# Four buffers instead of two for the routed experts' loads and stores, loads issued six blocks ahead

## The chip, the cores and the metric

The kernel runs on one core of a Trainium2 chip. A core has TensorE (PE: matrix products, into PSUM banks), VectorE (DVE), ScalarE (ACT), GpSimd (POOL) and SyncE (SP), which here only issues DMAs, and 16 DMA engines that serve all queues. Engines run their own instruction lists and wait for each other by semaphores. The metric is the device time of one launch in microseconds. Before the change it is 1456.23 us, the median of 3 runs (1455.55 to 1457.21).

## What is computed

One transformer block on x of shape 32 x 256 x 128 (32 sequences, 8192 tokens), float32. The modulation comes from c. First a gated linear attention with 16 heads adds to x, then a mixture of experts with 8 routed experts (top 2 per token) and one shared expert. Cut to what matters here:

```
h = layernorm(x) * (1 + cb) + sb
shared   = (silu(h @ shared_gate.T) * (h @ shared_up.T)) @ shared_down.T
probs    = sigmoid(h @ router_w.T + routing_bias)
scores, indices = top_k(probs, 2);  scores = scores / sum(scores)
w[t, indices[t]] += scores[t]
g = silu(h @ gate_w[e]);  u = h @ up_w[e]
combined = sum over e of  w[:, e] * ((g * u) @ down_w[e])
x = x + gb * (shared + combined)
```

Hidden size H = 128, expert width I = 256. Only a token's two chosen experts have a weight other than zero, and the kernel computes only those.

## The kernel before, in words

**Attention and routing (to about 1062 us).** The attention runs over 32 sequences. Behind it the routing of a pair of sequences at a time normalises, scores and picks the two experts, and POOL scatters each token's row (128 values of h, the token's slot and a mark) with indirect DMAs into rows_dram, which has a region for every expert. SP waits for all of these scatters before it goes on. `ga_all` holds the attention's output gate for all sequences; POOL's `update_x` is its last reader.

**The block table (1062 to 1076 us).** DVE works out, from how many rows each expert has received, a table of 39 blocks of 512 rows (`BLOCKS` = 2 x 8192 / 512 + 7): for every block the expert and the first row. SP reads it with register loads. Blocks beyond an expert's rows hold padding.

**The routed experts, 39 blocks.** All engines run the same pipeline over the blocks, and each has its own loop, whose body has two blocks (`two_units` on ACT and DVE):

- SP: `load_rows(i)` reads the block's row number and loads 260 KB of rows into `erows`; `load_gate_up(i)` reads the expert and loads gate and up weights (128 KB each) into `ew_in`; `load_down(i)` loads the down weights (128 KB) into `ed_in`. `load_ahead(i)` issues rows i+2, gate and up i+2, down i+1. The row load waits for `s_hx` and `s_yr` of block i (transposed, row numbers read), the gate and up load for `s_ewl` of block i, the down load of i+1 for `s_dn` of block i-1 (its down projection is done). These waits are L323.
- PE: `rows_transposed(i+2)` (four transposes, L1315), `gate_up_block(i+1)` (twelve products of 512 columns, three passes of split float32, L1318 to L1320), `down_block(i)` (L1580).
- ACT: `high_weights` and `high_h` round weights and rows to the high part, `silus` applies silu, `copy_y_out` (L814) copies the down projection's PSUM bank to `y_out`, once the scatter that last used that half has landed.
- DVE: `split_block` computes the low parts and the row numbers (`y_rows`, L1235), `gate_times_up` multiplies (L1228), `y_rows_out` (L1242) converts the row numbers into `y_row`, once the scatter two blocks back has landed.
- POOL: `scatter_y(i)` waits for `s_yo` and `s_id` and issues four indirect DMAs (L635) that write 128 rows each into y_dram.

Every buffer that a load or a store touches has two halves: `erows`, `ew_in`, `ed_in`, `y_out`, `y_known` and `y_row`. They lie in `pairs`, which the attention has left by then. The halves for PSUM banks, for the split parts and for `act` are two as well.

**The shared expert (from about 1370 us).** 16 steps of 512 tokens. SP waits until all scatters to y_dram have landed (L426), then loads the rows of y back, DVE combines them with the shared expert's result, POOL applies the gate and adds to x, SP stores.

The order of the work is written out by hand; there is no planner.

Of the kernel before, what the change touches and what calls it, by code (L numbers as in the profile page):

```python
# [21 lines left out]
BLOCKS = TOP * TOKENS // STEP + E - 1  # L22
# [12 lines left out]
def block_kernel(nc, x, W_q, W_k, W_v, W_gate, b_gate, W_o, shared_gate, shared_up, shared_down,  # L35
# [11 lines left out]
    with ctx:  # L47
# [3 lines left out]
        def sem(name):  # L51
# [31 lines left out]
        gb_all = sb("gb_all", [P, B, D])  # L83
        h_all = sb("h_all", [P, TOKENS])
# [20 lines left out]
        block_rows = sb("block_rows", [P, REGION // STEP])  # L105
# [19 lines left out]
        past_blocks = shared[:, 512:512 + BLOCKS * E].rearrange("p (i e) -> p i e", e=E)  # L125
        filled = shared[:, 1024:1024 + E * (REGION // STEP)].rearrange("p (e m) -> p e m", e=E)
# [38 lines left out]
        y_known = sb("y_known", [P, 2, ST])  # L165
        y_row = sb("y_row", [P, 2, ST], i32)
# [37 lines left out]
        s_ce, s_cs, s_cT_ps, s_cT = sem("c_exp"), sem("c_silu"), sem("cT_psum"), sem("cT_ready")  # L204
        s_mod_ps, s_mod = sem("mod_psum"), sem("mod_ready")
# [5 lines left out]
        s_whi, s_wsplit, s_guhi, s_gusplit = sem("w_high"), sem("w_split"), sem("gu_high"), sem("gu_split")  # L211
# [28 lines left out]
        s_rin, s_win, s_din, s_ysc, s_yin = ([sem(f"{n}_{u}") for u in range(2)] for n in (  # L240
            "rows_in", "weights_in", "down_in", "y_scattered", "y_loaded"))
# [8 lines left out]
        (s_xr, s_fc, s_fz, s_fst, s_fmv, s_fve, s_frs, s_fxn, s_fT, s_fh, s_fw, s_fp, s_fa, s_fq, s_fs, s_fb,  # L250
         s_fcl, s_fv, s_fqs, s_fo, s_fot, s_fy, s_fyg, s_fx) = (sem("seq_" + n) for n in (
            "x_reloaded", "selectors", "zeros", "stats", "moments", "variance_eps", "rstd", "xn", "xT_psum", "h",
# [8 lines left out]
        AGAIN = ROUNDS  # L261

# [4 lines left out]
        def _(sp):  # L267
# [118 lines left out]
            def load_rows(i, u):  # L386
                if not (isinstance(i, int) and i < 2):
                    alone(s_hx, i - 1)
                    alone(s_yr, i - 1)
                row = sp.value_load(block_i[0:1, 0, ds(i, 1)], min_val=0, max_val=ROWS - STEP)  # L390
                sp.dma_start(erows[:, u, :, :], rows_dram[ds(row, STEP), :].rearrange("(p n) c -> p n c", p=P)).then_inc(s_rin[u], 16)

            def load_gate_up(i, u):
                if not (isinstance(i, int) and i < 2):
# [5 lines left out]
            def load_down(i, u):  # L400
                if not (isinstance(i, int) and i < 2):
# [4 lines left out]
            for i in range(2):  # L406
                load_rows(i, i)
                load_gate_up(i, i)
            load_down(0, 0)

            def load_ahead(i, u):
                load_rows(i + 2, u)
                load_gate_up(i + 2, u)
                load_down(i + 1, 1 - u)

            load_ahead(0, 0)
            load_ahead(1, 1)
# [3 lines left out]
            load_ahead(BLOCKS - 3, 0)  # L421
            load_down(BLOCKS - 1, 0)

            sp.wait_ge(s_ysc[0], 64 * (BLOCKS // 2 + 1))
            sp.wait_ge(s_ysc[1], 64 * (BLOCKS // 2))
# [25 lines left out]
        def _(pool):  # L451
# [34 lines left out]
            counted(block_rows[:, :], [[STEP, REGION // STEP]], 0, 0).then_inc(s_const, 1)  # L486
# [117 lines left out]
            with growing(pool):  # L604
# [11 lines left out]
                with pool.Fori(0, B) as b:  # L616
                    alone(s_fmv, b + 1)
                    g.tensor_scalar(veps[:, :], mv[:, :, 1], EPS, None, ALU.add).then_inc(s_fve, 1)
                    alone(s_fve, b + 1)
# [10 lines left out]
            def scatter_y(v, u):  # L630

                alone(s_yo, v + 1)
                alone(s_id, v + 1)
                for n in range(ST):
# [4 lines left out]
            with pool.Fori(0, BLOCKS // 2) as k:  # L639
                scatter_y(k * 2, 0)  # L640
                scatter_y(k * 2 + 1, 1)
            scatter_y(BLOCKS - 1, 0)
# [17 lines left out]
        def _(sc):  # L660
            a = nc.scalar
            sc.wait_ge(s_c, 16)
            a.activation(c_e, c_in, ACT.Exp, scale=-1.0).then_inc(s_ce, 1)
# [50 lines left out]
            for k, m in enumerate(W_ORDER):  # L714
# [5 lines left out]
                if k == 2:  # L720
                    sc.wait_ge(s_mod, 1)
                    h_attention(0, 1)
# [66 lines left out]
            def high_weights(v, u, k):  # L789
                if not (isinstance(k, int) and k == 0):  # L790
                    sc.wait_ge(s_u, v * 2 - 2)
                sc.wait_ge(s_win[u], k * 32 + 32)
                a.activation(ew_hi[:, u, :, :].rearrange("p m n -> p (m n)"), ew_in[:, u, :], ACT.Copy).then_inc(s_ewh, 1)

            def high_h(v, u, k):
                sc.wait_ge(s_hx, v + 1)
                if not (isinstance(k, int) and k == 0):
                    sc.wait_ge(s_u, v * 2 - 2)
                a.activation(eh_hi[:, u, :], HX[u][:, :], ACT.Copy).then_inc(s_ehh, 1)
# [5 lines left out]
            def silus(v):  # L805
                for i in range(IT):
                    sc.wait_ge(s_g, v * 2 + i + 1)
                    a.activation(silu[:, i, :], GU[i][0][:, :], ACT.Silu).then_inc(s_silu, 1)

            def copy_y_out(v, u, k):  # L810
                sc.wait_ge(s_dn, v + 1)
                if not (isinstance(k, int) and k == 0):
                    sc.wait_ge(s_ysc[u], k * 64)
                a.activation(y_out[:, u, :, :], DN[u][:, :].rearrange("p (n d) -> p n d", n=ST), ACT.Copy).then_inc(s_yo, 1)  # L814

            high_weights(0, 0, 0)
            high_h(0, 0, 0)
            high_weights(1, 1, 0)
            high_h(1, 1, 0)
            silus(0)  # L820

            def two_units(k):
                high_weights(k * 2 + 2, 0, k + 1)
                high_h(k * 2 + 2, 0, k + 1)
                silus(k * 2 + 1)
                copy_y_out(k * 2, 0, k)
                high_weights(k * 2 + 3, 1, k + 1)
                high_h(k * 2 + 3, 1, k + 1)
                silus(k * 2 + 2)
                copy_y_out(k * 2 + 1, 1, k)  # L830

            two_units(0)
            with sc.Fori(1, BLOCKS // 2 - 1) as k:
                two_units(k)
            high_weights(BLOCKS - 1, 0, BLOCKS // 2)
            high_h(BLOCKS - 1, 0, BLOCKS // 2)
# [819 lines left out]
```

## Time and profile before

| | |
|---|---|
| median of 3 runs | 1456.23 us (1455.55 to 1457.21) |
| profiled execution, its own time | 1459.87 us |
| its span | 1458.10 us |
| granted TensorE clock, mean | 0.957 |
| busy: PE, PEld, DVE, ACT, POOL | 89%, 74%, 75%, 56%, 64% |

The profile is one execution. Its page cuts the span into 40 slices of 36.5 us and gives the busy tenths of each engine:

```profile
PE   6999999999999999999999999999138767787796
DVE  8888889898898988989898998987133433433387
ACT  5666666666666666666666676665023333333342
POOL 3444776867677686776867677676725555555555
PEclk9999999999999999999999999999559988989898
```

A digit of 9 is 90% busy or more. Slices 1 to 28 are attention and routing, slice 29 and part of 30 the block table and the first loads, slices 31 to 37 the routed experts, the last ones the shared expert. PEclk is the clock that TensorE was granted, in tenths of full speed. SPq is SP's own queue of instructions: in the chain of waits a line SPq is time that SP spent in that instruction, "issue" time for which the profile shows no one waited for, "remote" or "another core or an unknown queue" a release whose origin the profile doesn't name. A window's row has start:end, its length, busy us (and number) of PE, PEld, DVE, ACT and POOL, the mean granted clock, the share of the DMA engines, and GB/s.

### The profile page before, as it was taken

How to read it: one execution, taken by the hardware profiler on the slowest of the kernel's cores; microseconds unless marked ns; L12 is line 12 of the kernel's file. 1: busy time of each engine (PE TensorE's matmuls, PEld its weight loads, DVE VectorE, ACT ScalarE, POOL GpSimd, SP SyncE). 2: the span in 40 equal slices, each digit the busy share in tenths (PEclk: the TensorE clock that was granted, in tenths of full speed). 3: DMA queues.
4: the chain of work that ended last, by engine and by line, in shares of the span. 5: the costliest groups of instructions: out<-in, count | busy, mean ns of one | idle time of the engine just before them, and what ended most of it. 6: DMA issues, size and time to landing. Idle time of an engine off the chain costs nothing.

```text
span 1458.1 us, 38072 instructions
## 1 busy us (share of the span) xinstructions
PE 1298.9 (89%) x10935; PEld 1072.5 (74%) x10935; DVE 1094.8 (75%) x3120; ACT 812.4 (56%) x2061; POOL 927.0 (64%) x1426
## 2 busy tenths in 40 slices
PE   6999999999999999999999999999138767787796
PEld 5888788888888788888878888787027656676686
DVE  8888889898898988989898998987133433433387
ACT  5666666666666666666666676665023333333342
POOL 3444776867677686776867677676725555555555
PEclk9999999999999999999999999999559988989898
DMA  8902020202112020220202112020224434443154
GB/s 240 259 7 81 2 96 0 95 16 78 40 55 95 6 89 20 75 90 5 95 15 80 34 61 95 4 92 23 103 81 125 130 114 125 122 124 117 50 168 144
DMA packets 94721, 118.46 MB, mean 81 GB/s; under 512 B 9668, under 2 KB 60535, under 8 KB 94672
## 3 DMA queue, kind: packets, MB, share of 16 engines
q1 hardware_dynamic: 85584, 100.93, 22.1%
q0 software_dynamic: 9088, 16.94, 3.5%
q8 instruction: 23, 0.38, 0.1%
q14 instruction: 26, 0.21, 0.1%
HBM read 50.13 MB, written 61.08 MB: 76 GB/s over the span
## 4 chain that ended last, share of the span: by engine, by line
PE 50%; DVE 22%; issue 13%; SPq 7%; POOL 2%; DMA 2%; DVEq 1%; ACT 1%; another core or an unknown queue 1%; POOLq 0%; ACTq 0%
PE head_banks L1394 10%; PE bank L1405 8%; PE bank L1415 6%; DVE pairs L1048 5%; PE bank L1318 5%; PE bank L1319 5%; PE bank L1320 5%; DVE pairs L1044 4%; DVE A L1070 3%; DVE pairs L1053 2%; SPq L384 2%; PE bank L1356 2%; PE bank L1357 2%; PE bank L1358 2%; DVE xn L887 1%
## 5 line engine op out<-in xcount | busy, mean ns | idle before, releaser
L635 POOL DMA_INDIRECT y_dram<-pairs,y_row x156 | 155.0, 994 | 147.3 <-issue 124.9
L1318 PE MATMUL bank<-h_hi,big 128*128 128x256 f32 x768 | 237.2, 309 | 3.4 <-DVE h_lo L895 2.8
L1044 DVE TENSOR_TENSOR_SCAN pairs<-pairs 128x128 f32<-128x128 f32 x512 | 232.2, 494 | 4.4 <-issue 1.7
L1394 PE MATMUL head_banks<-pairs 64*128 64x128 f32 x2048 | 225.9, 297 | 5.3 <-DVE A L1070 3.2
L1405 PE MATMUL bank<-A,shared 128*64 128x256 f32 (+1 forms) x2048 | 223.0, 339 | 0.0
L1048 DVE TENSOR_TENSOR_SCAN pairs<-pairs,cap 128x128 f32<-128x128 f32 x512 | 219.8, 469 | 0.0
L1319 PE MATMUL bank<-h_lo,big 128*128 128x256 f32 x768 | 216.8, 282 | 0.0
L1320 PE MATMUL bank<-h_hi,big 128*128 128x256 f32 x768 | 216.4, 282 | 0.0
L463 POOL TENSOR_SCALAR_AFFINE_SELECT A<-A 128x256 f32<-128x256 f32 x256 | 113.7, 444 | 154.5 <-ACT A L744 153.4
L1394 PEld LDWEIGHTS head_banks<-pairs 64*128 64x128 f32 x2048 | 155.6, 186 | 62.6 <-issue 42.5
L1070 DVE COPY_PREDICATED A<-causal,head_banks 128x384 f32<-128x384 int32 x256 | 150.2, 587 | 63.4 <-PE head_banks L1394 62.2
L541 POOL TENSOR_SCALAR pairs<-pairs 128x256 f32<-128x256 f32 x256 | 118.0, 461 | 102.5 <-ACT pairs L674 99.7
L744 ACT ACTIVATE A<-head_banks 128x384 f32<-128x384 f32 x256 | 125.3, 490 | 101.9 <-PE head_banks L1394 101.8
L1415 PE MATMUL bank<-wo,shared 128*128 128x128 f32 x1024 | 182.0, 300 | 0.0
L1405 PEld LDWEIGHTS bank<-A,shared 128*64 128x64 f32 x2048 | 124.2, 136 | 67.9
L534 POOL DMA_INDIRECT rows_dram<-token_rows,dest x128 | 130.5, 1019 | 58.2 <-issue 48.1
L1415 PEld LDWEIGHTS bank<-wo,shared 128*128 128x128 f32 x1024 | 133.4, 190 | 43.7 <-issue 43.7
L1318 PEld LDWEIGHTS bank<-h_hi,big 128*128 128x128 f32 x768 | 146.0, 190 | 4.9 <-DVE h_lo L895 3.2
L1319 PEld LDWEIGHTS bank<-h_lo,big 128*128 128x128 f32 x768 | 145.8, 190 | 0.0
L1320 PEld LDWEIGHTS bank<-h_hi,big 128*128 128x128 f32 x768 | 145.5, 189 | 0.0
L688 ACT ACTIVATE shared<-bank 128x256 f32<-128x256 f32 x256 | 98.4, 384 | 65.4 <-PE bank L1405 61.2
L674 ACT ACTIVATE pairs<-bank,half_bg 128x256 f32<-128x256 f32 x256 | 120.1, 469 | 21.6 <-PE bank L1320 8.5
(193 smaller groups left out, 2816.3 us busy)
## 6 DMA issues: line engine op xcount, KB each, us to landing
rows_dram<-pad_row SPq DMA_DIRECT2D x17, 2080.0 KB, 8.2
pairs<-rows_dram SPq DMA_DIRECT2D x39, 260.0 KB
pairs<-y_dram SPq DMA_DIRECT2D x16, 512.0 KB, 3.8
pairs<-in_L_ffn_gate_w_dram SPq DMA_DIRECT2D x39, 128.0 KB
pairs<-in_L_ffn_up_w_dram SPq DMA_DIRECT2D x39, 128.0 KB
pairs<-in_L_ffn_down_w_dram SPq DMA_DIRECT2D x39, 128.0 KB
token_rows<-new_rows SPq DMA_DIRECT2D x16, 260.0 KB, 2.3
mod_rows<-mod_rows_dram SPq DMA_DIRECT2D x32, 128.0 KB, 3.2
```

The source lines that it names most:

```text
L534: g.indirect_dma_start(rows_dram, bass.IndirectOffsetOnAxis(ap=dest[:, m:m + 1], axis=0), token_rows[:, m % PT, :], None, bounds_check=ROW ...
L635: g.indirect_dma_start(y_dram, bass.IndirectOffsetOnAxis(ap=y_row[:, u, n:n + 1], axis=0), y_out[:, u, n, :], None, bounds_check=TOKENS * ...
L744: a.activation(A[:, p % 2, 1, :, :], S[:, 1, 0:3 * P].rearrange("p (c t) -> p c t", c=3), ACT.Copy).then_inc(s_ax, 1)
L1044: v.tensor_tensor_scan(F[:, par, cols], ga_t[:, par, cols], ga_t[:, par, cols], 1.0, ALU.mult, ALU.min)
L1048: ins = v.tensor_tensor_scan(G[:, par, cols], gi_t[:, par, cols], cap[:, :], 1.0, ALU.mult, ALU.min)
L1070: v.copy_predicated(A[:, p % 2, 0, :, :].rearrange("p c t -> p (c t)"), causal[:, :, :].bitcast(i32).rearrange("p c t -> p (c t)"), S[:, 0 ...
L1318: t.matmul(dst, hi, m_hi, start=True, stop=False)
L1319: t.matmul(dst, hi, m_lo, start=False, stop=False)
L1320: return t.matmul(dst, lo, m_hi, start=False, stop=True)
L1394: last = t.matmul(S[:, h, c * P:(c + 1) * P], keys[rows, :], queries[rows, :], start=True, stop=True)
L1405: last = t.matmul(O[h * DK:(h + 1) * DK, k * P:T], v_sb[:, k, vcols], blocks.rearrange("p c t -> p (c t)"), start=(k == 0), stop=(k == CHU ...
L1415: last = t.matmul(Y[:, k * D:(k + 1) * D], oT[:, p % 2, k * P:(k + 1) * P], wo[:, p, :], start=(p == 0 and k == 0), stop=(p == PAIRS - 1), ...
```

## The change

The block size gets a name of its own, `BLOCK`, and stays at 512. Everything that a block loads or stores has four buffers (`RING` = 4) in place of two: `erows`, `ew_in`, `ed_in`, `y_out`, `y_known`, `y_row`, with four semaphores each for loads and scatters. `erows` and `ed_in` move from `pairs` into `ga_all`. What is split, multiplied or kept in PSUM keeps its two halves (`half` = j % 2). A helper `unit(k, j)` names block k * 4 + j, its ring place, its half and how often the place was used before. The loop bodies of all five engines cover four blocks.

SP's loads for rows, gate and up are issued six blocks ahead of the down projection that the same point of the list waits for, the down weights four; a load waits until block i-4, which used its buffer last, is done with it. The first six blocks' rows, gate and up weights and the first four down weights are issued one after the other. To stay within the number of semaphores, some short chains of steps that had a semaphore for each step share one (the modulation, the split of the shared expert's weights, the moments in the branch for growing states). The core of the diff:

```
+BLOCK = 512
+RING = 4
-        ew_in = pairs[:, 0:1024].rearrange("p (u n) -> p u n", u=2)
-        ed_in = pairs[:, 1024:1536].rearrange("p (u i d) -> p u i d", u=2, i=IT)
-        erows = pairs[:, 1536:2576].rearrange("p (u n c) -> p u n c", u=2, n=ST)
-        y_out = pairs[:, 2576:3600].rearrange("p (u n d) -> p u n d", u=2, n=ST)
+        ew_in = pairs[:, 0:2048].rearrange("p (u n) -> p u n", u=RING)
+        y_out = pairs[:, 2048:2048 + RING * BT * D].rearrange("p (u n d) -> p u n d", u=RING, n=BT)
+        after = ga_all[:, :, :].rearrange("p b d -> p (b d)")
+        erows = after[:, 0:RING * BT * ROW].rearrange("p (u n c) -> p u n c", u=RING, n=BT)
+        ed_in = after[:, 3072:4096].rearrange("p (u i d) -> p u i d", u=RING, i=IT)
...
+        TURNS = (BLOCKS - 3) // RING
+        def unit(k, j):
+            return k * RING + j, j % RING, j % 2, k + j // RING
+        def begun(turn):
+            return not (isinstance(turn, int) and turn == 0)
...
-            def load_rows(i, u):
-                if not (isinstance(i, int) and i < 2):
-                    alone(s_hx, i - 1)
-                    alone(s_yr, i - 1)
+            def load_rows(k, j):
+                i, u, _, turn = unit(k, j)
+                if begun(turn):
+                    alone(s_hx, i - (RING - 1))
+                    alone(s_yr, i - (RING - 1))
...
-                    alone(s_ewl, i - 1)
+                    alone(s_ewl, i - (RING - 1))
...
-                    alone(s_dn, i - 1)
+                    alone(s_dn, i - (RING - 1))
...
-            with sp.Fori(1, BLOCKS // 2 - 1) as k:
-                load_ahead(k * 2, 0)
-                load_ahead(k * 2 + 1, 1)
+            for i in range(RING):
+                load_rows(0, i)
+                load_gate_up(0, i)
+                if i >= 1:
+                    load_down(0, i - 1)
+            load_down(0, RING - 1)
+            for i in (RING, RING + 1):
+                load_rows(0, i)
+                load_gate_up(0, i)
+            with sp.Fori(0, TURNS - 1) as k:
+                for j in range(RING):
+                    load_rows(k, j + RING + 2)
+                    load_gate_up(k, j + RING + 2)
+                    load_down(k, j + RING)
...
-                if not (isinstance(k, int) and k == 0):
-                    alone(s_ysc[u], k * 64)
+                if begun(turn):
+                    alone(s_ysc[u], turn * 16 * BT)
```

The last pair is `y_rows_out` on DVE; `copy_y_out` on ACT changes in the same way. PE's `rows_transposed`, `gate_up_block` and `down_block` keep their order: rows of block v+2, gate and up of v+1, down of v.

## Rows read from the trace of the kernel before

**Rows 1.** Windows: length, busy time by engine (columns told above), PEclk, DMA, GB/s.

```profile
1094.00:1376.00 282.00, 220.52 (x1245) 189.71 (x1244) 108.24 (x226) 105.51 (x194) 155.00 (x156) 0.92 0.38 113
...
1392.00:1438.00 46.00, 46.00 (x284) 40.96 (x283) 41.49 (x114) 18.30 (x30) 28.19 (x20) 1.00 0.56 168
```

**Rows 2.** Waits, 1094 to 1376: us in total, times, longest us.

```profile
DVE y_row L1242 <- DMA y_dram<-pairs,y_row: 59.4, 20, 5.7
PE bank L1315 <- DMA pairs<-rows_dram: 55.7, 24, 6.7
ACT pairs L814 <- remote: 50.4, 15, 4.8
```

**Rows 3.** The same view of SP's queue, 1094 to 1376.

```profile
SPq L323 <- PE head_banks L1580: 6.8, 5, 3.8
SPq L323 <- remote: 4.7, 3, 1.6
SPq L323 <- PE bank L1580: 3.8, 3, 2.7
```

**Rows 4.** The chain of waits by line, 1094 to 1376.

```profile
by line: issue 35.1%; SPq L384 10.4%; SPq L390 6.1%; SPq L391 4.3%; SPq L404 4.1%; DMA pairs<-rows_dram 4.0%; SPq L397 3.9%; PE head_banks L1580 2.8%; PE bank L1318 2.7%; another core or an unknown queue 2.7%; SPq L398 2.6%; PE bank L1320 2
```

**Rows 5.** SP's DMA issues in order of time: start us, us, line.

```profile
1083.61 0.34 SPq L391 DMA_DIRECT2D pairs<-rows_dram  x1
1086.34 0.38 SPq L404 DMA_DIRECT2D pairs<-in_L_ffn_down_w_dram  x1
1087.61 0.33 SPq L391 DMA_DIRECT2D pairs<-rows_dram  x1
...
1093.71 0.38 SPq L404 DMA_DIRECT2D pairs<-in_L_ffn_down_w_dram  x1
1095.70 0.35 SPq L391 DMA_DIRECT2D pairs<-rows_dram  x1
...
1122.01 0.38 SPq L404 DMA_DIRECT2D pairs<-in_L_ffn_down_w_dram  x1
1124.03 0.26 SPq L391 DMA_DIRECT2D pairs<-rows_dram  x1
```

**Rows 6.** SP's DMA issues in order of time, 1190 to 1206.

```profile
1195.17 0.01 SPq L404 DMA_DIRECT2D pairs<-in_L_ffn_down_w_dram  x1
1201.72 0.00 SPq L391 DMA_DIRECT2D pairs<-rows_dram  x1
```

**Rows 7.** A piece of the chain in order of time: start us, us, what.

```profile
1197.38 0.71 SPq L390
```

**Rows 8.** POOL in order of time, 1174 to 1206, idle before in brackets.

```profile
1178.62 0.97 POOL L635 DMA_INDIRECT y_dram<-pairs,y_row  x1 [3.40 <-issue]
...
1190.04 1.32 POOL L635 DMA_INDIRECT y_dram<-pairs,y_row  x1 [6.61 <-issue]
...
1199.33 0.97 POOL L635 DMA_INDIRECT y_dram<-pairs,y_row  x1 [0.30 <-issue]
```

**Rows 9.** Single lines, 1094 to 1376: ns min/median/max, first and last start.

```profile
L635 POOL DMA_INDIRECT y_dram<-pairs,y_row x156: 971/974/1320, 1094.4 to 1374.2; - x156
...
L391 SPq DMA_DIRECT2D pairs<-rows_dram x35: 3/264/725, 1095.7 to 1346.0; - x35
```

**Rows 10.** All engines in order of time, inside 1148 to 1172.

```profile
1150.62 0.97 POOL L635 DMA_INDIRECT y_dram<-pairs,y_row  x1 [2.48 <-issue]
...
1157.84 0.97 POOL L635 DMA_INDIRECT y_dram<-pairs,y_row  x1 [2.41 <-issue]
1158.00 1.95 PE L1580 MATMUL head_banks<-pairs,shared 128*128 128x128 f32 x16
...
1161.67 0.97 POOL L635 DMA_INDIRECT y_dram<-pairs,y_row  x1 [0.30 <-issue]
...
1163.67 0.60 ACT L814 ACTIVATE pairs<-head_banks 128x512 f32<-128x512 f32 x1 [4.51 <-remote]
...
1165.11 0.97 POOL L635 DMA_INDIRECT y_dram<-pairs,y_row  x1 [2.46 <-issue]
```

More of the change, by code:

```diff
@@ L384, in expert, with load_gate_up @@
                 return sp.value_load(block_i[0:1, 1, ds(i, 1)], min_val=0, max_val=E - 1)
-            def load_rows(i, u):
-                if not (isinstance(i, int) and i < 2):
-                    alone(s_hx, i - 1)
-                    alone(s_yr, i - 1)
[L390 to L394, printed above, removed]
-                    alone(s_ewl, i - 1)
+            def load_rows(k, j):
[3 more added lines that the diff above has]
+                    alone(s_yr, i - (RING - 1))
+                row = sp.value_load(block_i[0:1, 0, ds(i, 1)], min_val=0, max_val=ROWS - BLOCK)
+                sp.dma_start(erows[:, u, :, :], rows_dram[ds(row, BLOCK), :].rearrange("(p n) c -> p n c", p=P)).then_inc(s_rin[u], 16)
+            def load_gate_up(k, j):
+                i, u, _, turn = unit(k, j)
+                if begun(turn):
+                    alone(s_ewl, i - (RING - 1))
                 e = expert(i)
@@ L637, in scatter_y @@
                                          oob_is_err=False).then_inc(s_ysc[u], 16)
[L639 to L642, printed above, removed]
+            with pool.Fori(0, TURNS) as k:
+                for j in range(RING):
+                    scatter_y(k, j)
+            for j in range(3):
+                scatter_y(TURNS, j)
             pool.wait_ge(s_gb, 16)
@@ L811, in copy_y_out @@
                 sc.wait_ge(s_dn, v + 1)
[L812 to L836, printed above, removed]
-            silus(BLOCKS - 2)
-            copy_y_out(BLOCKS - 3, 0, BLOCKS // 2 - 1)
+                if begun(turn):
+                    sc.wait_ge(s_ysc[u], turn * 16 * BT)
+                a.activation(y_out[:, u, :, :], DN[half][:, 0:BT * D].rearrange("p (n d) -> p n d", n=BT), ACT.Copy).then_inc(s_yo, 1)
@@ new lines, in _, with turn_of_blocks @@
+            for j in range(2):
+                high_weights(0, j)
+                high_h(0, j)
+            silus(0, BLOCK)
+            def turn_of_blocks(k):
+                for j in range(RING):
+                    high_weights(k, j + 2)
+                    high_h(k, j + 2)
+                    silus(k * RING + j + 1, BLOCK)
+                    copy_y_out(k, j)
+            turn_of_blocks(0)
+            with sc.Fori(1, TURNS) as k:
+                turn_of_blocks(k)
+            high_weights(TURNS, 2)
@@ new lines, in _, with turn_of_blocks @@
+            split_block(0, 0)
+            split_block(0, 1)
+            gate_times_up(0, 0, BLOCK)
+            y_rows_out(0, 0)
+            def turn_of_blocks(k):
+                for j in range(RING):
+                    split_block(k, j + 2)
+                    gate_times_up(k * RING + j + 1, (j + 1) % 2, BLOCK)
+                    y_rows_out(k, j + 1)
+            turn_of_blocks(0)
+            with dve.Fori(1, TURNS) as k:
+                turn_of_blocks(k)
+            split_block(TURNS, 2)
@@ L1548, in _, with rows_transposed, gate_up @@
             pe.wait_ge(s_blk, 1)
-            def rows_transposed(v, u, k):
-                pe.wait_ge(s_rin[u], k * 16 + 16)
-                if not (isinstance(k, int) and k == 0):
+            def rows_transposed(k, j):
+                v, u, half, turn = unit(k, j)
+                pe.wait_ge(s_rin[u], turn * 16 + 16)
+                if not (isinstance(v, int) and v < 2):
                     pe.wait_ge(s_ehl, v - 1)
-                for n in range(ST):
-                    last = transpose(HX[u][:, n * P:(n + 1) * P], erows[:, u, n, 0:D], P)
+                for n in range(BT):
+                    last = transpose(HX[half][:, n * P:(n + 1) * P], erows[:, u, n, 0:D], P)
                 last.then_inc(s_hx, 1)
-            def gate_up(v, u, w_hi_of, w_lo_of):
+            def gate_up(v, u, w_hi_of, w_lo_of, width):
                 for i in range(IT):
@@ L1582, in down_project, with down_block @@
                 last.then_inc(s_dn, 1)
-            def down_block(v, u, k):
-                pe.wait_ge(s_din[u], k * 16 + 16)
+            def down_block(k, j):
+                v, u, half, turn = unit(k, j)
+                pe.wait_ge(s_din[u], turn * 16 + 16)
                 if not (isinstance(v, int) and v < 2):
                     pe.wait_ge(s_yo, v - 1)
-                down_project(v, u, ed_in[:, u, :, :])
+                down_project(v, half, ed_in[:, u, :, :], BT)
             def down_shared(j, u):
```

276 lines of the change are left out of this document (132 added, 144 removed).

## The prediction

> **What bounds the kernel now.** I read the windows first, then who waits for whom, then the DMA queue of SP, then the order of time inside a few blocks. The windows give the stage of the routed experts, 1094 to 1376: 282 us of a span of 1458.1, in which TensorE is busy for 220.52 us at a granted clock of 0.92 and POOL's scatters for 155.00 [rows 1]. No engine is full there, whereas the shared expert right after keeps TensorE busy all the time (46.00 of 46.00) [rows 1]. So the stage is bound by waits. The list of waits names three kinds: POOL waits to scatter, DVE waits for a scatter to land before it may overwrite y_row (59.4 us), and TensorE waits for the loads of rows (55.7 us) [rows 2]. A load is late because of who issues it: SP waited for other engines only 6.8 + 4.7 + 3.8 us, with two waits of 0.2 beside them 15.7 us, in the whole stage [rows 3]. The rest is SP's own instruction stream: "issue" and SPq lines make up most of the chain here, rows_dram's transfers 4.0% [rows 4].
>
> SP's stream runs at two speeds. Before the first scatter a block costs it 4.00 us (row load to row load, 1083.61 to 1087.61) [rows 5]. While POOL scatters, small SP instructions cost up to 0.7 us each [rows 7]: from the down load at 1195.17 to the next row load at 1201.72 SP takes 6.55 us [rows 6], where the same step with the same loop turn takes 2.02 outside (1122.01 to 1124.03) [rows 5]; POOL was scattering without a gap from 1190.04 to 1200.3 [rows 8]. Over the stage the 35 row loads lie 1346.0 - 1095.7 = 250 us apart (the last starts at 1346.0 in the view), 34 intervals of 7.36 us [rows 9]. A block costs SP 7.36 us where the instructions need 4. POOL's four scatters a block take 4 x 1.28 us (1157.84 to 1161.67 is three of them [rows 10]), so SP spends some 5.1 of 7.36 us beside a scatter. The same slowness holds back what TensorE reports: the down projection that starts at 1158.00 takes 1.95 us, yet ACT copies it out at 1163.67, after 4.51 us of "remote", just after the scatter at 1161.67 has ended; the next scatter starts at 1165.11 [rows 10].
>
> **The change part by part.** The sum is made against the profiled execution: 1459.87 us, 1.77 us around the span; it is 3.64 us above the median of the runs shown, 1456.23.
>
> 1. SP's waits. Loads of block j waited for block j-2 to be done with the buffers; now they wait for block j-4, and the row load is issued two blocks ahead of the down weights. At most all 15.7 us of [rows 3] go. SP needs no less work for it, so the loads gain no more than that: an SP that never waits is still an SP at 7.36 - 15.7/34 = 6.9 us a block. Part of the waiting lay inside a scatter, where SP would have crept anyway. Bounds: 15.7 if all of it becomes full-speed work, 5 if it is worked off only at the crawling speed (2.02 us of work in 6.55, under a third: [rows 6] against [rows 5]). I take two thirds, 10.5, since most of these waits end when the scatter does.
>
> 2. The loop of SP turns once for four blocks instead of two. Down load to row load takes 2.02 us across the turn (1122.01 to 1124.03) and 1.27 without (1086.34 to 1087.61) [rows 5]: 0.75 us, some eight turns fewer, 6.0 us. Bounds: 0 if SP has nothing to lose there, 12 if the turns fall into scatters. I take 5, since part of a turn's time passes in waits.
>
> 3. The start. Row load 4 was issued at 1095.70 because the down load before it waited until 1093.71 [rows 5]. Now the order is rows 3, gate and up 3, down 2, down 3, rows 4, without a wait: 1087.61 + 2.73 (1083.61 to 1086.34) + 1.27 for one more down load (as long as the step from a down load to the next issue) + 1.27 (1086.34 to 1087.61) = 1092.9 [rows 5], 2.8 us earlier. Bounds 0 and 3; TensorE is also waiting for compute there. I take 2.5.
>
> 4. DVE's wait for the landing of the scatter two blocks back, 59.4 us [rows 2], and ACT's for y_out go: both now look four blocks back. What is late next is the down projection's report to ACT (50.4 us of "remote" [rows 2]) and the load of the rows. So this gives nothing of its own beside step 1: the chain holds SP and issue, not that wait [rows 4]. Bounds: 0 and a few us already inside rival A.
>
> 5. The buffers. erows and ed_in move into ga_all, whose last reader is the gating of the last batch, ahead of POOL's last scatter of the routing; SP waits for that scatter before it loads a row anyway. Cost 0; cover gone, it would be a wait of SP once, of a us. The five merged semaphores keep the order of their steps, on chains at the kernel's start: 0, within 0.5 us to either side. Block table, block size and number of transfers are as before: 39 blocks, four scatters each. The bodies of the block loops double on TensorE, ACT, DVE and POOL, which removes some turns of those too; their branch gaps are hidden behind waits: 0.
>
> Sum: 10.5 + 5 + 2.5 = 18.0 us. 1459.9 - 18 = 1441.9 profiled, less 3.64: 1438 us.
>
> A rule bears on step 1. The Trainium skill, DMA: Bandwidth & Descriptors, section "Issuing engines are not separate DMA queues", says that the time a sequencer takes to initiate a DMA is usually small beside the transfer. By that rule SP has room, and four buffers would take every landing off TensorE's path, as in rival A (1401). The trace disagrees: transfers are 4.0% of the chain, SP's lines and issue the most of it [rows 4]. The same page, "Rules for kernel authors", advises to issue early and wait late; no row before shows what that gives where the issuing itself is full.
>
> **The rivals.**
> A. TensorE becomes the bound. If SP's slow periods only hurt because nothing was in stock, six blocks of stock let TensorE run on. Then its wait for rows, 55.7 us [rows 2], goes, with step 3: 1459.9 - 55.7 - 2.5 - 3.6 = 1398; with 220.52 of 282 us busy [rows 1] there is no more than 61.5 to gain. For it: TensorE waits for rows in nearly every block. Against it: stock is only a loan, 39 blocks at 6.9 us of SP outlast a stock of six; and reports from TensorE come late during scatters [rows 10]. Taken together some 3 us less, 1401. Chance 0.19.
> B. Lockstep, no change. Three blocks running start their scatters 7.22 and 7.27 us apart, with gaps of 2.41 and 2.46 us [rows 10]: the down projection that ends inside a scatter is copied out only after it, 0.6 us, and the next scatter starts 0.8 us later. If this pace, not the loads, rules, 38 intervals of 7.25 are what is there now (155 scatter intervals in 279.8 us, 7.22 a block [rows 9]) and step 3 disappears in it: 1455. Chance 0.16.
> C. Slower. Four y_out buffers and y_row columns allow POOL to queue more blocks and scatter them without a gap, and in such a stretch SP creeps. After the pair from 1165.11 the next starts are 1178.62 and 1190.04 [rows 8, 10]: 24.93 us for three blocks, 8.31 each against 7.22. It decides once more than a third of the blocks fall in such triples beyond today's: 13 x 1.09 = 14 us, less the 2.5 of the start and nothing from steps 1 and 2: 1456.2 + 11.5 = 1468. All blocks so: 1456.2 + 38 x 1.09 = 1498. Against it: with loads as the limit, blocks come singly and POOL has no queue. Chance 0.16.
> That the loads don't go ahead at all, since SP never gets ahead of TensorE, is the forecast with step 1 at its low bound, 1444.
>
> **How the numbers follow.** Forecast 1438, own range 1428 to 1447 (steps at their bounds), chance 0.49; A 0.19, B 0.16, C 0.16. A change of 0.2%, 2.9 us, is about what a measurement of this kernel can tell. Faster: the forecast and A, and a fifth of B's cases: 0.71. Same: most of B, 0.12. Slower: C and a little of B, 0.17. The range reaches over A to 1397 and over C to 1468.
>
> **What would show it.** Step 1: SP's waits for other engines near 0 instead of 15.7, and the row loads still some 6.9 us apart, with 0.7 us pieces during scatters. Step 2: loop turns of SP at half the number. Step 3: row load 4 near 1092.9 and row load 5 near 1096. Step 4: no DVE wait at L1242's counterpart. The routed stage should end near 1358. It is wrong if the row loads come 5.5 to 6 us apart and TensorE no longer waits for them (A), if scatters keep starts 7.2 to 7.3 us apart with loads landed long before (B), or if triples of gapless scatters are followed by holes of 6 us and more (C).

## The result, and the profile after

The kernel after takes 1437.09 us (median of 4, 1435.78 to 1443.91), the kernel before 1455.89 beside it (median of 4): a ratio of 0.9878, 95% interval 0.985 to 0.9905. The forecast was 1438. Measured again later, beside a new measurement of before, the kernel after gave 1439.05 against 1453.63, ratio 0.989 (0.9857 to 0.9922). The profiled execution of after is the longest of its own, 1443.91 us, with a span of 1442.2.

The windows of after, columns as in [rows 1], the routed experts and then the shared expert:

```profile
1094.00:1358.00 264.00, 216.63 (x1247) 184.16 (x1246) 105.33 (x225) 102.11 (x189) 158.64 (x156) 0.95 0.40 118
1374.00:1420.00 46.00, 46.00 (x284) 40.94 (x284) 40.85 (x111) 18.32 (x30) 26.90 (x20) 1.00 0.55 162
```

The stage is 18 us shorter, and the shared expert fills TensorE as before. TensorE's granted clock is 0.95 where it was 0.92, and the same matmuls are busy 3.9 us less. The waits, as in [rows 2]; L1340 is what L1315 was, L841 what L814 was:

```profile
ACT pairs L841 <- remote: 68.8, 16, 7.1
...
PE bank L1340 <- DMA ga_all<-rows_dram: 12.4, 10, 3.3
```

DVE's wait at y_row is gone from the view, TensorE's for rows fell from 55.7 to 12.4 us, and ACT's for the report of the down projection grew from 50.4 to 68.8, the longest from 4.8 to 7.1. In SP's queue no wait for another engine is left in the stage, where [rows 3] had 15.7 us. The chain by line, as in [rows 4], has less issue, but no less of SP (L399 and L406 are the old L384 and L390):

```profile
by line: issue 31.5%; SPq L399 13.0%; another core or an unknown queue 6.7%; SPq L406 6.6%; SPq L407 5.3%; SPq L422 4.7%; SPq L414 4.6%; PE bank L1607 3.7%; SPq L415 3.3%; PE head_banks L1607 2.8%; PE bank L1343 1.9%; POOL y_dram L658 1.6%;
```

SP's row loads, as in [rows 5] and [rows 9]:

```profile
1085.76 0.33 SPq L407 DMA_DIRECT2D ga_all<-rows_dram  x1
...
1090.87 0.35 SPq L407 DMA_DIRECT2D ga_all<-rows_dram  x1
...
1094.45 0.30 SPq L407 DMA_DIRECT2D ga_all<-rows_dram  x1
```

```profile
L407 SPq DMA_DIRECT2D ga_all<-rows_dram x34: 3/238/703, 1094.5 to 1322.4; - x34
```

From row load 3 to row load 4 it is 5.11 us instead of 8.09. The 34 of the stage are (1322.4 - 1094.5) / 33 = 6.91 us apart instead of 7.36.

The view that shows best what changed and what did not is POOL's, grouped: busy us and mean ns, then idle before. Ahead of it stands the same row of before, which no group has:

```profile
L635 POOL DMA_INDIRECT y_dram<-pairs,y_row x156 | 155.0, 994 | 147.3 <-issue 124.9 <-ACT pairs L814 22.1 <-DVE y_row L1242 0.3
```

```profile
L658 POOL DMA_INDIRECT y_dram<-pairs,y_row x156 | 159.5, 1022 | 126.0 <-issue 103.6 <-ACT pairs L841 22.4
```

A train is here a stretch of POOL's scatters with no gap of more than 0.6 us. Between two scatters of one train lie 0.30 us each; over 150 scatters that is 45 us. What "issue" holds beyond it are the holes between trains: 80 us before, 59 after. From the first scatter's start to the last one's it was 279.8 us and is 263.2: 21 us less of holes, 4.5 us more of scatters (155.0 and 159.5). The 22 us behind ACT are the wait for the first block and stay.

Where the time that is left goes shows in the order of time, 1146 to 1162 in after:

```profile
1146.47 1.32 POOL L658 DMA_INDIRECT y_dram<-pairs,y_row  x1 [2.96 <-issue]
...
1151.21 1.95 PE L1607 MATMUL head_banks<-ga_all,shared 128*128 128x128 f32 x16
...
1155.81 0.97 POOL L658 DMA_INDIRECT y_dram<-pairs,y_row  x1 [0.30 <-issue]
...
1158.27 0.60 ACT L841 ACTIVATE pairs<-head_banks 128x512 f32<-128x512 f32 x1 [6.95 <-remote]
1159.70 1.32 POOL L658 DMA_INDIRECT y_dram<-pairs,y_row  x1 [2.92 <-issue]
```

The down projection ends at 1151.21 + 1.95 = 1153.16. POOL scatters two blocks in one train, from 1146.47 to 1156.78. ACT copies the projection out at 1158.27, 5.1 us after it was done and 1.5 us after the last scatter; and only then does POOL get work, after a hole of 2.92 us. From train to train it is 1159.70 - 1146.47 = 13.2 us, 6.6 a block. Seven such trains follow each other from 1106.6 on, with rows landed ahead of their use. Later in this execution the stock is used up, TensorE waits for rows again (the 12.4 us) and a block takes some 6.9.

Trains of two blocks are not new, there are only more of them. Counted from POOL's rows, the 156 scatters stood in 30 trains before, nine of them of two blocks without a gap, and [rows 10] shows the holes of 2.4 us after single blocks. After has 27 trains with twelve pairs, its second profiled execution 23 with sixteen.

Nor does every scatter hold a report back. Here one gets through at once, 0.03 us after the matmuls are done (1270.79 + 2.05 = 1272.84), while the second scatter of a train runs:

```profile
1270.79 2.05 PE L1607 MATMUL bank<-ga_all,shared 128*128 128x128 f32 x16
...
1272.37 0.97 POOL L658 DMA_INDIRECT y_dram<-pairs,y_row  x1 [0.30 <-issue]
...
1272.87 0.60 ACT L841 ACTIVATE pairs<-bank 128x512 f32<-128x512 f32 x1 [0.99 <-PE bank L1607]
```

Of the eleven down projections of after that end less than 3.4 us into a train, nine are copied out after 0.03 us. Of those that end later in one, all but one wait, 0.9 to 5.3 us, in some cases in part for ACT's other work.

### The profile page after: what moved, and what is told of

Its sections match the earlier page's. It is cut to its first block, busy times and chain, and to the rows that moved or that the text cites. A ratio compares the mean times of both kernels' runs of the same rounds, so it can differ in the third digit from the quotient of the medians.

```text
span 1442.2 us, 37915 instructions
## 1 busy us (share of the span) xinstructions
PE 1296.3 (90%) x10935; PEld 1067.6 (74%) x10935; DVE 1090.2 (76%) x3120; ACT 811.4 (56%) x2061; POOL 931.4 (65%) x1426
## 4 chain that ended last, share of the span: by engine, by line
PE 48%; DVE 23%; issue 13%; SPq 9%; POOL 2%; another core or an unknown queue 1%; DMA 1%; DVEq 1%; ACT 1%; POOLq 0%; ACTq 0%
PE head_banks L1419 10%; PE bank L1430 8%; PE bank L1440 6%; DVE pairs L1071 5%; DVE pairs L1067 5%; PE bank L1343 5%; PE bank L1344 5%; PE bank L1345 4%; DVE A L1093 3%; SPq L399 3%; DVE pairs L1076 2%; PE bank L1381 2%; PE bank L1383 2%; PE bank L1382 2%; DVE xn L910 1%
## 5 line engine op out<-in xcount | busy, mean ns | idle before, releaser
L658 POOL DMA_INDIRECT y_dram<-pairs,y_row x156 | 159.5, 1022 | 126.0 <-issue 103.6
```

What stands on the lines that cost most here:

```text
L658: g.indirect_dma_start(y_dram, bass.IndirectOffsetOnAxis(ap=y_row[:, u, n:n + 1], axis=0), y_out[:, u, n, :], None, bounds_check=TOKENS * ...
```

## The experiments

Each ratio is to the kernel before, measured again beside each group of experiments: 1455.74 us for e1 to e4, 1451.33 for e5 to e8, 1453.63 for e9 to e12. Times of different groups are compared by their ratios. "Holes" is the idle "issue" of POOL's scatters less 45 (less 42 with a pause, one of whose gaps is its own); "trains" counts POOL's trains; "rows" is TensorE's wait for the loads of rows inside 1094 to 1400. The two executions of after differ by 8 us of holes, so a smaller difference in that column says little. e3, e6, e11 and e12 stand in the text.

| kernel | median us | ratio (interval) | holes | trains | rows |
|---|---|---|---|---|---|
| before | | 1 | 80 | 30 | 55.7 |
| after | 1437.09 | 0.9878 (0.985 to 0.9905) | 59 | 27 | 12.4 |
| e9_after_again | 1439.05 | 0.989 (0.9857 to 0.9922) | 51 | 23 | 0 |
| e1_lead2 | 1450.79 | 0.9965 (0.9947 to 0.9982) | 65 | 29 | 46.5 |
| e2_stores2 | 1441.81 | 0.9915 (0.9896 to 0.9934) | 58 | 26 | 0 |
| e4_down_by_act | 1444.37 | 0.9935 (0.9918 to 0.9952) | 65 | 26 | 0 |
| e5_no_down | 1433.48 | 0.9878 (0.9851 to 0.9904) | 45 | 21 | 0 |
| e8_one_expert | 1435.38 | 0.9893 (0.9874 to 0.9913) | 46 | 22 | 0 |
| e7_pause | 1424.54 | 0.9815 (0.979 to 0.9839) | 5 | 6 | 7.9 |
| e10_pause_and_one_expert | 1423.26 | 0.9786 (0.9757 to 0.9815) | 2 | 3 | 0 |

**The lead taken back.** Four buffers and loops of four stay, the loads wait for block i-2 again and come in the old order.

```
-                if begun(turn):
-                    alone(s_hx, i - (RING - 1))
+                if past_two(i):
+                    alone(s_hx, i - 1)
```

> Four buffers everywhere and loops of four blocks, but each load waits again for block i-2 and is issued in the old order (rows and gate/up two ahead, down one ahead). Theory SP (SyncE's own instruction stream paces the stage, and the change mainly took its waits away): the waits of SP on other engines come back (some 15 us against 0), the saving of 19 us shrinks to the loop turns and the start, so about 1448 to 1453. Rival stores (what helped was that DVE and ACT no longer wait for a scatter to land): the time stays near 1437, since the four store buffers are still there.

Measured 1450.79 us (12 runs, 1446.13 to 1454.68). This is where the theory had it (1448 to 1453), and not the 1437 of the rival. SP's waits are back, in the view of [rows 3] 24.9 us with two smaller ones (before had 15.7), and its last row load is no longer early (1333.5, in after 1322.4):

```profile
SPq L341 <- remote: 13.8, 8, 5.6
SPq L341 <- PE bank L1606: 6.1, 5, 2.7
```

The lead with its new start is worth 0.989 - 0.9965 = 0.0075, 11 us, or 13 by the first measurement of after. What remains, 5 us (3 to 8), is that of loops of four and of the four store buffers together; the two were not taken apart.

**Only the stores' lead taken back.** ACT and DVE wait for the scatter two blocks back.

```
-                if begun(turn):
-                    alone(s_ysc[u], turn * 16 * BT)
+                if not (isinstance(m, int) and m < 2):
+                    alone(s_ysc[(j - 2) % RING], (k + (j - 2) // RING + 1) * 16 * BT)
```

> The changed kernel, but ACT's copy to y_out and DVE's y_row wait again for the scatter two blocks back to land; loads stay six ahead. Theory SP: those waits lie beside SP's pace and cost nothing or little, 1437 to 1441. Rival stores: they return in full, 59 us of DVE waits of which a third or more is on the path, 1448 to 1456.

```profile
DVE y_row L1268 <- DMA y_dram<-pairs,y_row: 73.8, 18, 5.2
```

1441.81 us, 0.8 above the theory's range and 6 below the rival's. DVE waits 73.8 us for landings, more than the 59.4 of [rows 2], and it costs 0.0025 to 0.0037, 4 to 5 us, with intervals that touch those of after. TensorE no longer waits for rows here, yet the time is no better.

**The indirect scatters taken away.** One plain DMA per block; the placement of the rows is left out.

```
-                for n in range(BT):
-                    g.indirect_dma_start(y_dram, ..., y_out[:, u, n, :], ...)
+                g.dma_start(y_dram[ds(v * BLOCK, BLOCK), :].rearrange("(p n) d -> p n d", p=P), y_out[:, u, :, :])
```

> The four indirect scatters of a block are replaced by one plain DMA of the same 256 KB from POOL's queue, written block by block, so the placement by token is left out and the output is not the reference's. Theory SP: no scatters, no creeping; a block costs SP some 4.2 us instead of 6.9, TensorE's 5.5 to 5.8 us become the bound, its reports come at once, and the stage shrinks by some 1.1 us a block: 1437 - 39 x 1.1 = 1394 (1385 to 1405). Rival traffic (SP and the reports are slowed by the DMA traffic of the stage, not by the indirect scatters): bytes are the same, so it stays above 1425.

Measured 1366.83 us (2 runs), ratio 0.9398 (0.9373 to 0.9422): 27 us below the expected 1394 and 18 below its range. The window of the stage, columns as in [rows 1], and three issues of SP:

```profile
1094.00:1290.00 196.00, 195.49 (x1255) 175.69 (x1253) 107.20 (x233) 105.11 (x193) 20.98 (x39) 1.00 0.58 174
```

```profile
1200.48 0.33 SPq L407 DMA_DIRECT2D ga_all<-rows_dram  x1
1205.31 0.33 SPq L407 DMA_DIRECT2D ga_all<-rows_dram  x1
1209.55 0.33 SPq L407 DMA_DIRECT2D ga_all<-rows_dram  x1
```

This is rival A's kernel: TensorE is busy 195.49 of 196.00 us at a clock of 1.00. The same 39 blocks have 21 us less of PE time than in after, and SP's row loads are 4.2 to 4.8 us apart, not 6.9. Both slow things, SP's stream and the late reports, go away with the indirect scatters; the bytes stored are the same, so the rival of traffic is out. The plain DMA is also one issue a block in place of four, and which of the two matters was not tried.

**SP relieved, three ways.** ACT issues the down loads; or those of block 4 and later are left out, so that the weights are old ones; or the loads of a block go together behind one read of its expert, all four blocks ahead instead of six.

```
+            def load_down(k, j):        # on ACT
+                e = sc.value_load(block_i[0:1, 1, ds(i, 1)], min_val=0, max_val=E - 1)
+                sc.dma_start(ed_in[:, u, :, :], down_w[ds(e, 1), :, :]...)
```

```
-                    load_down(k, j + RING)
```

```
-                    load_rows(k, j + RING + 2)
-                    load_gate_up(k, j + RING + 2)
-                    load_down(k, j + RING)
+                    load_rows(k, j + RING)
+                    load_weights(k, j + RING)
```

> The changed kernel with the down weights' loads of blocks 4 and later issued by ACT right behind its copy of the down projection, instead of by SP. Nothing else. Theory SP: SP has a fifth to a quarter less to issue, its pace falls from 6.9 to some 5.5 us, the stock lasts, and the stage runs at the pace seen while the stock lasts in the changed kernel (pairs of scatter starts 5.5 and 7.7 us apart, 6.6 a block): 25 blocks x 0.3 us = 7 us less, 1428 to 1433. Rival: SP is no longer a limit in the changed kernel, the time stays at 1437 or rises with ACT's added instructions, up to 1445.

> The changed kernel without the loads of the down weights of blocks 4 to 38 (the buffers keep the first four blocks' weights, so the result is not the reference's). SyncE has a fifth to a quarter less to issue and no other engine has more. Theory two limits (the scatters' train sets a pace of 6.6 us a block by holding back TensorE's reports, SyncE's own pace of 6.9 is felt only once the stock is used up): the stock lasts, all 38 intervals run at 6.6 to 6.7, 1428 to 1433. Theory SP alone (SyncE paces the stage and everything else has room): 6.9 falls to 5.7, 1395 to 1405. Neither: 1437 if loads are not on the path at all.

> The changed kernel with one register load of the expert per block instead of two: rows, gate, up and down weights of a block are issued together, all four blocks ahead, which saves SyncE some 0.5 of 4.2 us a block and costs two blocks of lead. Output as the reference's. Theory two limits: SyncE's pace falls from 6.9 to about 6.3, below the 6.6 of the scatters, 1430 to 1435. If the lead of six matters more than the instructions saved, 1437 to 1445.

1444.37, 1433.48 and 1435.38 us. The first missed its range by 11 us and fell into that of its rival, in which SP is no longer a limit and ACT pays for the added instructions. The other two lie 0.5 and 0.4 us above the ranges of two limits (1428 to 1433, 1430 to 1435); SP alone would have given 1395 to 1405 in the second. In none of the three does TensorE wait for rows, and without the down loads SP's last row load of the stage starts at 1298.8, 24 us earlier than in after:

```profile
L654 POOL DMA_INDIRECT y_dram<-pairs,y_row x156 | 160.1, 1026 | 114.0 <-issue 89.6 <-ACT pairs L837 24.4
```

The row is that of the kernel without the down loads. Its holes are 45 us instead of 59 and 51 in the two executions of after. By the ratios it is 0 to 2 us faster than after, and the one with a single read 0 to 2 us slower. The intervals leave room for some 5 us, and in these two traces it is 252.6 and 253.0 us from the first scatter to the last, less than in after (263.2 and 258.8). So SP's stream is at most a small part of what sets the time of after. It hides behind the reports: the repeated run of after shows that too, where one execution got through with TensorE never waiting for rows and was no faster (1438.0 us of span). With ACT as issuer the loads cost ACT a hole of its own, ahead of its next copy:

```profile
1201.38 0.60 ACT L837 ACTIVATE pairs<-head_banks 128x512 f32<-128x512 f32 x1 [2.73 <-PE head_banks L1611]
1202.14 0.40 ACTq L847 DMA_DIRECT2D ga_all<-in_L_ffn_down_w_dram  x1
1202.70 0.63 ACT L814 ACTIVATE big<-pairs 128x512 fp32r<-128x512 f32 x1 [0.72 <-issue]
```

By the ratios that kernel is 7 to 8 us slower than after. That this hole is the whole of it was not tried.

**A scatter more per block.** A fifth indirect scatter with row numbers out of bounds, which writes nothing.

```
+                g.indirect_dma_start(y_dram, bass.IndirectOffsetOnAxis(ap=nowhere[:, 0:1], axis=0),
+                                     y_out[:, u, 0, :], None, bounds_check=TOKENS * TOP - 1, oob_is_err=False).then_inc(s_ysc[u], 16)
```

> The changed kernel with a fifth indirect scatter in every block whose indices all lie out of bounds, so that it writes nothing and costs POOL its 1.28 us. Theory two limits: the train of scatters sets the pace, so the whole cost is on the path: 1437 + 39 x 1.28 = 1487 (1480 to 1495), with intervals of some 8 us. Theory SP alone: POOL stands idle 1.7 us a block, SyncE creeps a little longer; at most half of it shows, 1445 to 1465.

1489.53 us, ratio 1.027 (1.0243 to 1.0297), inside the range of two limits. All of it is paid, though TensorE never waits for rows. Pairs of blocks are now ten scatters and a hole of three:

```profile
1200.38 0.60 ACT L846 ACTIVATE pairs<-head_banks 128x512 f32<-128x512 f32 x1 [7.71 <-remote]
1201.82 1.31 POOL L660 DMA_INDIRECT y_dram<-pairs,y_row  x1 [2.99 <-issue]
...
1217.78 1.32 POOL L660 DMA_INDIRECT y_dram<-pairs,y_row  x1 [3.11 <-issue]
```

1217.78 - 1201.82 = 15.96 us a pair, against 13.2 in after: 1.4 a block, 52 us over 38 blocks. By the ratios it is 0.038 to 0.039, 55 to 57 us.

**A pause in the train.** POOL writes a buffer that no one needs between the second and the third scatter of each block.

```
+                    if n == 2:
+                        alone(s_pool, v + 40)
+                        g.memset(wo[:, :, :], 0.0).then_inc(s_pool, 1)
```

> The changed kernel with a memset of 128x1024 on POOL (some 1 us) between the second and the third scatter of every block. Theory two limits, with reports let through in the pause: TensorE's report comes out in the middle of a block's scatters instead of 1 us behind its end, the gap of 2.2 us between blocks shrinks by as much as the pause costs, 1432 to 1445. If the pause lets nothing through, it adds its whole length, 1437 + 39 x 1 = 1476.

1424.54 us (4 runs, 1423.62 to 1426.05), 0.9815, 7 us below the expected 1432 to 1445: POOL has more to do, and by the ratios the kernel is 9 to 11 us faster than after. It is as much faster than the two kernels with SP relieved, measured beside it (1433.48 and 1435.38). In order of time:

```profile
1159.97 0.98 POOL L661 DMA_INDIRECT y_dram<-pairs,y_row  x1 [0.30 <-issue]
...
1160.93 0.99 POOL L660 MEMSET wo<- 128x1024 f32 x1
...
1161.76 0.60 ACT L844 ACTIVATE pairs<-bank 128x512 f32<-128x512 f32 x1 [3.54 <-remote]
1161.79 1.95 PE L1610 MATMUL head_banks<-ga_all,shared 128*128 128x128 f32 x16
1162.09 0.97 POOL L661 DMA_INDIRECT y_dram<-pairs,y_row  x1 [0.17 <-issue]
```

```profile
L661 POOL DMA_INDIRECT y_dram<-pairs,y_row x156 | 158.1, 1014 | 69.9 <-issue 46.7 <-ACT pairs L844 21.6 <-DVE y_row L1271 0.9
```

0.8 us into the memset the report reaches ACT. That is no single case: 23 of the 39 copies begin 0.5 to 1.1 us after a memset has begun. The y_out of the next block is ready before the train ends, and the holes are all but gone. The account closes to some 2 us: 54 us of holes go, 39 pauses come of 0.84 us each (the scatters around one start 2.12 us apart, not 1.28), 33 us, which leaves 21; from the first scatter's start to the last it is 243.7 us (1095.5 to 1339.2) where after had 263.2 in its longest execution. Against the other execution of after, with 258.8, the holes leave 46 - 33 = 13 where 15.1 was measured. Now SP is late at times: TensorE waits 7.9 us for rows.

**The pause with SP relieved.** The pause, and the loads of a block together behind one read of its expert.

> The memset of 128x1024 between the second and third scatter of each block, and the loads of a block issued together with one read of its expert. Two close limits (the train of scatters holds TensorE's reports; SP's own stream, which the pause left on the path, since its row loads landed 0.4 us before their use): with both lifted a block takes 6.0 to 6.2 us in place of 6.29 with the pause alone, over 38 blocks 4 to 11 us: 1414 to 1421 us, ratio 0.974 to 0.979. Rival, in which the pause works because SP's instructions get through during it: SP had little left to gain, 1422 to 1427 us.

1423.26 us, 0.9786 (0.9757 to 0.9815), 15 us below after (1439.05 beside it, by the ratios). The time is the rival's, the ratio is the upper end of mine, so the trace has to decide. TensorE waits for no rows, and from first to last scatter it is 243.3 us (1093.2 to 1336.5), as with the pause alone. POOL's scatters, grouped and in order of time:

```profile
L646 POOL DMA_INDIRECT y_dram<-pairs,y_row x156 | 160.6, 1029 | 67.7 <-issue 43.7 <-ACT pairs L829 21.8 <-DVE y_row L1256 1.5
```

```profile
1203.88 0.97 POOL L646 DMA_INDIRECT y_dram<-pairs,y_row  x1 [0.17 <-issue]
...
1207.96 0.97 POOL L646 DMA_INDIRECT y_dram<-pairs,y_row  x1 [0.30 <-issue]
...
1208.92 0.97 POOL L645 MEMSET wo<- 128x1024 f32 x1
...
1210.06 0.97 POOL L646 DMA_INDIRECT y_dram<-pairs,y_row  x1 [0.17 <-issue]
```

POOL hardly stands idle between its first scatter and its last: 1210.06 - 1203.88 = 6.18 us a block are its own instructions. That is the third floor. The rival is right in that SP had little left to give. It is not right in its reason, that the pause works because SP's instructions get through during it: with SP relieved in both and TensorE never waiting for rows in either, the pause still takes the ratio from 0.9893 (0.9874 to 0.9913) to 0.9786, 15 us. And 26 of the 39 copies of ACT begin 0.5 to 1.1 us after a memset has begun. After again, as the mark for these:

> The kernel after the change, unaltered, so that the three kernels beside it have it as their mark on the same chip. Both theories: 0.985 to 0.991 of the kernel before in the same call, 1433 to 1440 us.

**Shape and place of the pause.** An eighth of the width; and the full one ahead of the first scatter.

```
-                        g.memset(wo[:, :, :], 0.0).then_inc(s_pool, 1)
+                        g.memset(wo[:, 0, 0:128], 0.0).then_inc(s_pool, 1)
```

```
-                    if n == 2:
+                    if n == 0:
```

> The memset between the second and third scatter made an eighth as wide (128x128 in place of 128x1024). If what helps is a stretch in which GpSimd does something other than a scatter, long enough for a report to be made (the report came 0.95 us after the memset of 0.99 us had begun), a short one lets less through: 1428 to 1436 us. If it is only that the train is cut at all, as much as with the long one: 1422 to 1426 us. If neither, and the added wait only delays: 1437 to 1442 us.

> The memset of 128x1024 ahead of the first scatter of each block in place of between the second and third. The report of the down projection of the next block falls due while scatters 1 to 3 of a block run, so a pause in their middle serves it and one at the start lets it through only where two blocks stand back to back, one block late; and there it delays the scatters whose y_out is ready by 1 us. Place matters: 1430 to 1442 us. Rival, in which any microsecond of pause per block is as good: 1422 to 1427 us.

1440.54 us, 0.9905 (0.9873 to 0.9937), and 1440.38 us, 0.9898 (0.9861 to 0.9935): neither gains anything. The first is the case in which neither cut nor length helps (1437 to 1442) and not the expected part of the gain, the second lies in its range. The short one, in order of time:

```profile
1199.66 0.97 POOL L661 DMA_INDIRECT y_dram<-pairs,y_row  x1 [0.30 <-issue]
1200.62 0.23 POOL L660 MEMSET wo<- 128x128 f32 x1
1201.02 0.97 POOL L661 DMA_INDIRECT y_dram<-pairs,y_row  x1 [0.17 <-issue]
...
1202.30 0.98 POOL L661 DMA_INDIRECT y_dram<-pairs,y_row  x1 [0.30 <-issue]
...
1204.68 0.60 ACT L844 ACTIVATE pairs<-bank 128x512 f32<-128x512 f32 x1 [6.99 <-remote]
```

0.39 us without a scatter (1200.63 to 1201.02) let this report through no more than the usual gaps; it came 1.4 us after the train's end. The full one, ahead of the first scatter:

```profile
1208.46 0.98 POOL L660 MEMSET wo<- 128x1024 f32 x1
...
1209.47 1.95 PE L1610 MATMUL head_banks<-ga_all,shared 128*128 128x128 f32 x16
...
1213.44 0.97 POOL L661 DMA_INDIRECT y_dram<-pairs,y_row  x1 [0.31 <-issue]
...
1215.41 0.60 ACT L844 ACTIVATE pairs<-head_banks 128x512 f32<-128x512 f32 x1 [6.07 <-remote]
```

In a train of two blocks this pause, too, stands in the middle, between the blocks. But the down projection starts only when it is over, ends at 1211.42 and is copied out 1.0 us after the train. So a cut alone is not enough, its length counts (0.23 us did nothing, 0.99 us did), and it must lie where the report falls due. In these two kernels TensorE waits 9.1 and 16.6 us for rows, so a small gain may hide behind SP.

## Why the prediction was right

**Step 1, SP's waits, 10.5 us.** They went in full, the row loads came 6.91 us apart where I had 6.9, and with step 3 (13.0 together) the lead is measured at 11 to 13. The size is right. The two thirds in it were a choice between two bounds, so that they hit this well is in part luck. The reason given for it is right only in part. I had SP's stream at 6.9 as the floor. It is one of two floors that lie close together, and with it gone the time hardly falls: with TensorE never short of rows (the kernels with SP relieved, and one execution of after) a block still costs 6.5 to 6.9 us. The sum had no second floor; that the two lie so near is luck for the forecast. What the early loads gave shows in POOL's trains: the next block's down projection is more often done while a block is being scattered, and trains of two blocks with one hole take the place of some trains of one with one each (29 trains without the lead, 27 and 23 with it). The counts differ little more than those of the two executions of after, so this last step is argued more than shown; what is measured is SP's waits back in the kernel without the lead, and TensorE's for rows (46.5 us).

**Step 2, half the turns, 5 us.** The kernel that keeps them and gives up the lead is 5 us faster than before (3 to 8). It also has the four store buffers, so the turns alone are not shown. The 2.02 us that I took for a turn outside a scatter were not outside one, POOL began to scatter in their middle, so the 0.75 us a turn is no clean price:

```profile
1122.76 0.97 POOL L635 DMA_INDIRECT y_dram<-pairs,y_row  x1 [2.56 <-issue]
```

**Step 3, the start, 2.5 us.** From row load 3 to row load 4: forecast 1092.9 - 1087.61 = 5.3 us, measured 5.11. The absolute 1090.87 is lower because row load 3 itself came 1.85 us earlier: row load 1 stood at 1078.16 instead of 1079.17, and the two steps from there took 7.60 us instead of 8.44.

**Step 4, the stores, 0.** The wait went. Taken back alone it costs 4 to 5 us with touching intervals, so my 0 was low, but inside its bound of a few us.

**Step 5, 0.** Nothing in the trace of after stands against it; it was not tried alone.

**Rival A.** TensorE as the bound needs the scatters gone; with stock alone it never came. By the rule of the Trainium skill, DMA: Bandwidth & Descriptors, "Issuing engines are not separate DMA queues", the time a sequencer takes to initiate a DMA is usually small beside the DMA itself. Here SP's issuing is 4.0 us a block where no scatter runs [rows 5] and 6.9 beside scatters. Still my use of the trace against it was too strong, since with the issuing off the path the time hardly moved.

**Rival B** had the mechanism and the wrong price. It put the held report at a pace of 7.25 us, which is that of single blocks in [rows 10]; with loads in stock the same mechanism runs in pairs at 6.6. It is the main bound of the kernel after, as the pause shows by lifting it. Worked out from [rows 10] the pair was 8 x 1.28 us and 2.1 more for the hole, 12.3 us or 6.2 a block, and would have been a second bound in the sum.

**Rival C.** More trains of two blocks came, with holes of 2.9 us and not 6.6. SP crept in them and was ahead by then.

TensorE's clock, 0.92 to 0.95, stood in no step. The stage's matmuls are busy 3.9 us less; how much of that is in the 19 us is open.

## What to carry to other kernels

When a wait for loads goes, ask how the next-longest wait looks in the new rhythm, not in the old one: a hole after each block may become one after each second. Count an engine's holes (idle less its usual gap per instruction) before and after, in more than one execution; they show what an edit did when two limits lie close together. And where reports come late beside indirect scatters, try a stretch of a microsecond without one, at the point where a report falls due.
